# The second attention of a transformer block: GpSimd normalizes x in place of VectorE

## What is computed

```
x = x + attention_a(layernorm(x))      # 16 heads of 8, causal, three heads with weighted keys
x = x + ffn(layernorm(x))              # 128 -> 512 -> 512 -> 512 -> 128
x = x + attention_b(layernorm(x))      # 16 heads of 8, rotary positions, no mask
x = x + ffn(layernorm(x))

def _layernorm(x, axis=-1, eps=1e-05):
    m = jnp.mean(x, axis=axis, keepdims=True)
    v = jnp.var(x, axis=axis, keepdims=True)
    return (x - m) / jnp.sqrt(v + eps)
```

## Time and profile before

| | |
|---|---|
| median of 3 runs | 2544.91 us (2537.69 to 2549.25) |
| profiled execution: time | 2543.48 us |
| profiled execution: span, first to last instruction | 2541.7 us |
| TensorE, VectorE, ScalarE, GpSimd busy | 84%, 68%, 58%, 39% of the span |
| first attention, about | 0 to 820 us |
| first feed-forward, about | 820 to 1255 us |
| rotary attention, about | 1255 to 2096 us |
| second feed-forward, about | 2096 to 2542 us |

### The profile page before, as it was taken

The page is one execution under the profiler, slowest core; times in us unless marked ns, Lnnn a source line. Parts: engine busy times, 40 slices in busy tenths (PEclk is TensorE's granted clock), DMA queues, the critical chain, the costliest instruction groups (busy, mean ns, idle before and its releaser), DMA issues. The chain is left out here.

```text
span 2541.7 us, 37867 instructions
## 1 busy us (share of the span) xinstructions
PE 2136.9 (84%) x13378; PEld 972.0 (38%) x13378; DVE 1725.2 (68%) x2589; ACT 1485.3 (58%) x2980; POOL 982.1 (39%) x1184
## 2 busy tenths in 40 slices
PE   1989888888888599999648998999899875999998
PEld 0323223223222377777411222222222211777776
DVE  5777656666653367666268989998998851666664
ACT  0366556556556255655306777777777773556565
POOL 2445445445433255544332232242233200445544
PEclk8799878878878699999858999999999996999999
DMA  6343433433431000000033344334434310000000
GB/s 169 81 90 79 102 83 76 104 83 75 103 83 25 15 1 1 1 1 1 25 81 70 75 95 90 76 80 94 83 74 102 81 30 15 5 13 14 9 13 17
DMA packets 114577, 147.03 MB, mean 58 GB/s; under 512 B 27728, under 2 KB 88656, under 8 KB 113232
## 3 DMA queue, kind: packets, MB, share of 16 engines
q1 hardware_dynamic: 114384, 144.54, 26.0%
HBM read 78.40 MB, written 66.06 MB: 57 GB/s over the span
## 5 line engine op out<-in xcount | busy, mean ns | idle before, releaser
L586 DVE TENSOR_REDUCE b_negmax<-ps_max 128x2 f32<-128x1024 f32 x512 | 612.0, 1220 | 93.6 <-PE ps_max L700 91.0
L667 ACT ACTIVATE b_prob<-ps_score 128x512 f32<-128x512 f32 x1024 | 547.8, 598 | 202.2 <-PE ps_score L687 200.9
L586 DVE TENSOR_REDUCE a_negmax<-ps_max 128x2 f32<-128x256 f32 (+3 forms) x512 | 410.9, 821 | 225.3 <-PE ps_max L704 220.8
L667 ACT ACTIVATE a_prob<-ps_score 128x512 f32<-128x512 f32 (+3 forms) x1024 | 386.1, 437 | 297.7 <-PE ps_score L687 296.1
L687 PE MATMUL ps_score<-b_stack_q,stack_k 50*128 50x512 bf16 x1024 | 260.2, 392 | 55.5 <-ACT b_prob L667 46.1
L503 POOL TENSOR_SCALAR_AFFINE_SELECT a_prob<-a_prob 128x512 f32<-128x512 f32 x256 | 162.7, 635 | 361.5 <-ACT a_prob L667 361.5
L721 PE MATMUL ps_out<-b_prob,b_v_aug 128*9 128x512 f32 x2048 | 272.1, 604 | 18.7 <-ACT b_o_raw L640 12.7
L981 PE MATMUL ps_score<-fa_h,w_hi 128*128 128x512 f32 x1024 | 251.9, 400 | 29.8 <-DVE fa_h L895 28.8
L981 PE MATMUL ps_score<-fb_h,w_hi 128*128 128x512 f32 x1024 | 249.8, 398 | 28.6 <-DVE fb_h L895 27.6
L700 PE MATMUL ps_max<-stack_k,b_stack_q 48*128 48x512 bf16 x1024 | 233.8, 397 | 36.0 <-DMA stack_k<-d_stack 20.0
L687 PE MATMUL ps_score<-a_stack_q,stack_k 50*128 50x512 bf16 (+3 forms) x1024 | 203.5, 340 | 65.4 <-DMA a_stack_q<-d_nm 59.9
(11 more groups left out here) (139 smaller groups left out, 2946.7 us busy)
## 6 DMA issues: line engine op xcount, KB each, us to landing
stack_k<-d_stack SPq DMA_DIRECT2D x128, 192.0 KB, 4.8
d_stack<-a_parts SPq DMA_DIRECT2D x64, 192.0 KB, 2.8
a_stack_q<-d_stack SPq DMA_DIRECT2D x64, 192.0 KB, 4.5
d_stack<-b_parts SPq DMA_DIRECT2D x64, 192.0 KB, 2.8
b_stack_q<-d_stack SPq DMA_DIRECT2D x64, 192.0 KB, 4.4
d_stack<-a_parts SPq DMA_DIRECT2D x64, 128.0 KB, 2.8
d_stack<-b_parts SPq DMA_DIRECT2D x64, 128.0 KB, 2.8
d_stack<-a_parts SPq DMA_DIRECT2D x64, 64.0 KB, 2.5
```

The costliest lines, as they stand in the source:

```text
L586: dve.tensor_reduce(m["negmax"][:, t, :, p], dve_banks("max", k)[:, :, 0:keys], AX.X, ALU.max, negate=True).then_inc(s["max"], 1)
L667: act.activation(m["prob"][u % PROBS][:, g, lo:S], act_bank("score", 4 * u + g)[:, 0:S - lo], ACT.Exp).then_inc(s["prob"], 1)
```

## The change

In the rotary attention alone, `norm_apply` is called on GpSimd in unit 1, behind `norm_rstd` of unit 0, and no longer on VectorE in unit 2. VectorE keeps the statistics. The helper's parameter is renamed; its waits and its four instructions are the same. In the first attention and in the feed-forward stages VectorE normalizes as before. Line numbers behind L520 move by 2.

```
-def norm_apply(dve, m, s, b):
+def norm_apply(eng, m, s, b):
 
-    dve.wait_ge(s["rstd"], b + 1)
-    wait(dve, s["xT_ps"], b)
+    eng.wait_ge(s["rstd"], b + 1)
+    wait(eng, s["xT_ps"], b)
     for t in range(T):
-        last = dve.tensor_scalar(m["xhat"][:, t, :], m["x"][:, b, t, :], m["mv"][:, t, 0:1],
+        last = eng.tensor_scalar(m["xhat"][:, t, :], m["x"][:, b, t, :], m["mv"][:, t, 0:1],
                                  m["rstd"][:, t:t + 1], ALU.subtract, ALU.mult)
     last.then_inc(s["xhat"], 1)
...
                     if u == 0 and on(n, 0):
                         norm_rstd(pool, m, s, n)
+                    if u == 1 and on(n, 0) and rotary:
+                        norm_apply(pool, m, s, n)
                     if u == 2 and on(n, 1):
                         values(n - 1)
...
                         if u == 0:
                             norm_stats(dve, m, s, n)
-                        if u == 2:
+                        if u == 2 and not rotary:
                             norm_apply(dve, m, s, n)
```

## The result

| | before | with the change |
|---|---|---|
| median of 12 runs each, first comparison | 2548.97 us (2537.69 to 2561.89) | 2562.7 us (2546.89 to 2566.06) |
| ratio | | 1.0043, 95% interval 1.0022 to 1.0064 |
| second comparison, another chip (35 and 12 runs) | 2549.41 us | 2556.16 us, ratio 1.0021, interval 1.0006 to 1.0036 |
| profiled execution | 2543.48 us, span 2541.7 | 2561.64 us, span 2559.2 |

The ratios are those on record; they are not the quotients of the two medians, which would be 1.0054 and 1.0026. By the ratios the change costs some 5 to 11 us, by the medians 7 to 14. By the ratios that is under the half per cent that the prediction called no change, but the intervals exclude a gain and the time lies 12.7 us above the range's upper end. About 4 us of those 12.7 are the kernel before itself, whose median over more runs is 2549 and not 2544.9.

What follows compares the result with a forecast made beforehand. It took the pace of TensorE and ScalarE, not VectorE, as the bound in most steps. The terms, 0.2 - 1.0 + 0 = -0.8 us, gave 2542.7 from the profiled execution and 2544.1 from the median; forecast 2543, range 2536 to 2550.

Steps and rivals of the forecast that it cites:

- the half per cent: Whole kernel: about 0.5%, 13 us, is what a measurement can tell from no change; chance of the same time 0.91.
- the 14 steps: Rotary attention, steps 2 to 15: 1.02 us leaves VectorE in each, hidden by TensorE and ScalarE; value 0.
- The cover of 7.8 us: Middle steps: time from 1539.2 us to the transposes at 1547.02 that wait for xhat, 1.95 us per GpSimd instruction.
- Rival 1: VectorE is the bound after all; each step's 1.02 us is passed on, gain 15.3 us, giving 2528; chance 4%.
- rival 2: VectorE's reductions hold up GpSimd's four instructions; 14 steps lose 46 us, giving 2590; chance 3%.
- 331 ns, since tensor_scalar and cast both stream one tensor: Price of one 128x128 normalization on GpSimd: tensor_scalar's fixed part plus a cast's slope; four take 1.3 us.
- the term of step 0: Step 0, serial, nothing covers: four times 331 ns in place of 1.12 us, +0.2 us.
- The outer bound of 1.04 us: Upper price of one GpSimd normalization, from the power with 4 elements; +3.0 us in step 0.
- Step 1: VectorE sets the pace; TensorE's wait of 1.55 us returns to 0.52, and the gain of 1.0 us is kept.
- The sum: All terms of the rotary attention, step 0, step 1 and the covered steps: 0.2 - 1.0 + 0 = -0.8 us.
- the bounds of the sum: Whole sum: from -1.3 us to +3.0 us, the latter with the dearest instruction and nothing kept of step 1.
- Rival 3: The repeating 48.88 us step settles at another length; 0.3 us a step is 4 us, 2539 or 2548; chance 8%.

Runs made afterwards that it cites:

- e12: The kernel before with sixteen unread GpSimd instructions, eight forms twice, at the rotary attention's end; 2568.08 us beside 2550.63, one run each.
- e6: The change, but step 0 stays on VectorE and GpSimd normalizes from step 1; 2541.35 us, ratio 0.9989 to the kernel before.
- e3: The kernel before with 30 unread TensorE products in the rotary attention's step without maximum products; 2543.47 us, ratio 0.9977 to the kernel before.
- e4: The changed kernel with the same extra products as e3; 2545.16 us, ratio 0.9981 to the kernel before.
- e9: The kernel before with three unread normalizations on VectorE ahead of xhat in step 0, a pure delay; 2560.01 us, ratio 1.0021.
- e7: The kernel before with seven unread normalizations on VectorE ahead of xhat in step 0, a pure delay; 2552.05 us, ratio 1.0029.
- e10: e6 run again, unedited, in another comparison with the kernel before; 2545.28 us, ratio 0.9971.
- e5: The kernel before with the normalization on GpSimd in step 0 of the rotary attention alone; 2551.49 us, ratio 1.0023.

## Why the prediction was wrong

**What bounds the kernel, and the 14 steps: right.** Steps stayed at 48.88 us, the idle 0.23 us stayed, and TensorE never waited for xhat after step 0. The cover of 7.8 us took 3.1 us of normalization at more than twice its forecast price. Rival 1 (VectorE as the bound) and rival 2 (the reductions holding GpSimd up) did not occur: GpSimd's four took 3.12 us beside reductions and 3.13 in step 0, where VectorE stood still. The port rule of the Trainium skill's "SBUF — State Buffer", section "SBUF: two separate sides", which the prediction cited, agrees.

**"331 ns, since tensor_scalar and cast both stream one tensor": wrong by 2.4 times.** It is the term of step 0: +2.0 us and not +0.2. The outer bound of 1.04 us held it, the estimate didn't. What failed in this term is taking the slope from a cast, which has no arithmetic; alone it would have left the time inside the range. The Trainium skill's "GPSIMD Engine Reference", section "3.1 Elementwise — side-by-side cycle accounting", was read as support, with its 1.03 cycles an element for at most two operations; for the tensor_scalar here that figure does not hold: e12 shows 3.33 ns an element with two operations, and the measurement decides.

**Step 1: right in size.** -1.03 us, the wait gone and the chain behind it moved up with VectorE; e6 stands 1.0 us ahead of before at step 2 (79.6 against 80.6 us behind the head).

**The sum up to the last norm: about +1 us and not -0.8**, by the profiles (+1.0 and +0.3 at step 15) and by e3 and e4 (1.0 us in mean span, with a standard error of 0.9), of the wrong sign because of the price alone: 2.0 - 1.0 = +1.0. The 0.6 us outside the span were in no term.

**The step that failed was "the sum": a whole term was missing.** The prediction followed the moved instructions up to step 15 and stopped, which put everything behind it at nothing without a reason; "the bounds of the sum" knew no place where a shift of a few tenths could be worth ten. The last full step has no maximum products, and its clock can fall there: behind step 15 the change took 9.4 and 9.5 us more than before in the two pairs of profiles. The profile of before had the signs: a granted clock of 0.83 in that stretch, and products of 1.9 us from 2103.8 on. In the profiles of e9, e7 and the change, which delay step 0's transposes by 0.9, 1.9 and 2.1 us, the fall came 11, 11 and 21 us earlier in the work, worth 4 to 9.5 us of time; but it came 11 us earlier in e10 too, which has no delay, and no earlier in e5, which has one of 2.1 us. Rival 3 came nearest, in that it let the same work take another length, but it looked in the steady steps, and its 4 us were too few.

The page "TensorE: Matmul & The Clock Gate" of the Trainium skill, Part 1, says that recent activity of TensorE sets which of two levels it gets. The runs agree: the granted clock is 1.2 or 2.4 GHz in every profile and has no third value, and with more products in step 17 the higher one lasted to the step's end.

**Left open.** What makes the clock fall earlier in step 17 is not shown. The order by distance in eight profiled executions is an observation, with e5 and e12 against it, and one kernel met two falls (e6 and e10); that the place of the fall is partly chance, and the change only makes the early one more frequent, fits all profiles as well. A timed run without a profile doesn't tell where its clock fell, so the share of runs that met the early fall is unknown, and with it why the two comparisons of the same change give 1.0043 and 1.0021. The runs of the change do lie in two groups: in the first comparison seven of twelve took 2561.6 to 2566.1 us, with a mean granted clock of 0.899 to 0.903, and five 2546.9 to 2558.7 us, with 0.905 to 0.909. The profiled execution, with the early fall, is in the upper group. e10's profiled stage was longer than before's while its runs were faster, which shows how little one profile tells of the mean. What takes 0.6 us outside the span was not tried.

## What to carry to other kernels

Look where a pipelined stage drains: the steps in which one kind of TensorE work has already ended are where its clock can fall, and there a change that shifts the head by 1 or 2 us can cost several times as much (here 9.4 us behind a shift of 1.0 in one pair of profiles). Before a comparison of a few us is explained by the edit, read the granted clock of those steps in both traces, and if it differs, keep TensorE busy there with unread products in both kernels and compare again. A moved instruction is priced by one of its own kind, with as many operations and per-partition scalars; a cast is no stand-in for arithmetic on GpSimd.

## What the runs showed of the hardware

- GpSimd's tensor_scalar on 128x128 float32 with two operations and two per-partition scalars takes 797 ns (VectorE 0.34 us without contention), of which 75 ns for each such scalar; on 128x512 it takes 2077 ns.
- In step 17 of the rotary attention TensorE's clock fell 754.3, 750.9, 744.1 or 733.9 us behind its rise, each value repeated within 0.1 us in two or three executions; with before's code up to the stage's end it was 754.3 (twice) and 750.9 (e12).
- The later in the work it fell, the shorter the stage: 168.5, 163.1 to 163.7, 159.1 and 153 us from the last transposes to the stage's end, for falls 95, 106, 116 and 134 us behind them.
- Thirty unread products of 48x128x512 in a step of 48 us, in which TensorE waits for ScalarE's exponentials, made the kernel 0.23% faster (e3).
